# The first layer norm of an AdaLN block in its channel layout: row factors spread through DRAM in place of eight transposes, from the fourth batch on

## What is computed

```python
h = layernorm(x) * (1 + ca) + sa
u, gate = split(h @ W_in.T)
b_t  = u @ W_state.T
dt_t = minimum(softplus(u @ W_dt.T + b_dt), 10)
decay = exp(-dt_t * rate)
h_t = decay * h_t-1 + (1 - decay) * b_t          # scan over the 512 tokens
z = (h_t @ W_C.T) * silu(gate) + h * D
x = x + ga * (z @ W_out.T)
h = layernorm(x) * (1 + cb) + sb
xr, xk = mu_r * h + (1 - mu_r) * h_prev, mu_k * h + (1 - mu_k) * h_prev
x = x + gb * sigmoid(xr @ W_r) * (square(relu(xk @ W_k)) @ W_v)
```

## Time and profile before

| | us |
|---|---|
| median of 3 runs | 361.68 (361.56 to 362.54) |
| span of the profiled execution | 360.2 |
| PE busy | 353.1 (98%) |
| ACT busy | 306.8 (85%) |
| DVE busy | 302.7 (84%) |
| POOL busy | 256.5 (71%) |
| from scan to scan, batches 3 to 15 | 20.83 each |

### The profile page before, as it was taken

How to read it: one execution, slowest core, us unless ns; L and a number is a source line. 1 busy time by engine, 2 the same in 40 slices (tenths; PEclk the granted TensorE clock), 3 DMA queues, 4 the chain that set the end, 5 groups by cost and what they waited for, 6 DMA issues and landing times.

```text
span 360.2 us, 5599 instructions
## 1 busy us (share of the span) xinstructions
PE 353.1 (98%) x1680; PEld 277.3 (77%) x1680; DVE 302.7 (84%) x640; ACT 306.8 (85%) x422; POOL 256.5 (71%) x268
## 2 busy tenths in 40 slices
PE   8999899999999999999999999999999999999995
PEld 4667567788888888888888888888888888887654
DVE  3779997989989798988979898997989789768846
ACT  4677689799898989989898998989898998988484
POOL 2140849969696987969697796969789696766642
PEclk9999999999999999999999999999999999999999
DMA  8932130220413132040313104031301103010013
GB/s 289 405 119 70 46 119 0 88 90 0 136 40 116 59 104 74 13 146 18 118 60 116 60 35 139 4 116 59 119 0 58 61 0 118 0 61 1 0 58 117
DMA packets 13150, 29.15 MB, mean 81 GB/s; under 512 B 1216, under 2 KB 1984, under 8 KB 12992
## 3 DMA queue, kind: packets, MB, share of 16 engines
q1 hardware_dynamic: 12400, 28.32, 22.6%
q10 hardware_dynamic: 720, 0.48, 0.4%
HBM read 20.40 MB, written 8.39 MB: 80 GB/s over the span
## 4 chain that ended last, share of the span: by engine, by line
PE 91%; DVE 4%; ACT 2%; issue 2%; POOL 0%; ACTq 0%; DVEq 0%; POOLq 0%
PE slot L259 70%; PE slot L266 7%; PE slot L355 4%; PE slot L510 2%; PE slot L509 2%; PE slot L519 2%; PE slot L280 1%; PE slot L273 1%; ACT prev L636 1%; PE slot L363 1%; DVE xn L901 1%; PE slot L302 0%; DVE xk L935 0%; DVE stats L858 0%; DVE xr L935 0%
## 5 line engine op out<-in xcount | busy, mean ns | idle before, releaser
L1147 POOL TENSOR_TENSOR rstd<-mv,half_neg 128x4 f32<-128x4 f32 x16 | 16.1, 1009 | 44.8 <-DVE mv L873 44.8
L636 ACT ACTIVATE prev<-slot,mod,mix_prev 128x512 f32<-128x512 f32 x64 | 46.5, 790 | 1.1 <-PE slot L266 0.8
L259 PE MATMUL slot<-h_hi,wf_hi 128*128 128x512 f32 x120 | 44.0, 407 | 0.0
L1123 POOL TENSOR_TENSOR k_lo<-k_act,k_hi 128x512 fp32r<-128x512 f32 x30 | 38.2, 1297 | 7.7 <-ACT k_act L839 4.2
L1123 POOL TENSOR_TENSOR xk_lo<-xk,xk_hi 128x512 fp32r<-128x512 f32 x30 | 38.4, 1299 | 6.3 <-ACT xk_hi L664 6.3
L259 PE MATMUL slot<-h_hi,wf_lo 128*128 128x512 f32 x120 | 42.8, 397 | 0.0
L1166 POOL TENSOR_TENSOR h_lo<-h,h_hi 128x512 fp32r<-128x512 f32 x28 | 35.8, 1301 | 9.7 <-ACT h_hi L645 9.7
L1123 POOL TENSOR_TENSOR xr_lo<-xr,xr_hi 128x512 fp32r<-128x512 f32 x32 | 42.3, 1324 | 0.2 <-ACT xr_hi L670 0.2
L1217 POOL TENSOR_TENSOR z_lo<-z,z_hi 128x512 fp32r<-128x512 f32 x26 | 33.7, 1298 | 4.9 <-ACT z_hi L738 4.7
L957 DVE TENSOR_TENSOR slot<-silu,slot 128x1024 f32<-128x1024 f32 x16 | 19.7, 1230 | 20.0 <-PE slot L519 18.8
L259 PE MATMUL slot<-h_lo,wf_hi 128*128 128x512 f32 x120 | 35.1, 397 | 0.0
(11 more groups left out here) (157 smaller groups left out, 1009.7 us busy)
## 6 DMA issues: line engine op xcount, KB each, us to landing
x_ch<-x_ch_in SPq DMA_DIRECT2D x16, 512.0 KB, 3.8
x_tok<-x_tok_in SPq DMA_DIRECT2D x15, 512.0 KB, 3.5
x_out<-wmod SPq DMA_DIRECT2D x15, 512.0 KB, 3.0
wmod<-wmod_in SPq DMA_DIRECT2D x1, 1024.0 KB, 8.8
w_in<-weights_in SPq DMA_DIRECT2D x1, 1024.0 KB, 11.5
w_in<-weights_in SPq DMA_DIRECT2D x1, 512.0 KB, 4.5
wmod<-wmod_in SPq DMA_DIRECT2D x1, 512.0 KB, 5.7
x_tok<-x_tok_in SPq DMA_DIRECT2D x1, 256.0 KB, 3.2
```

Of the source, the lines that this page charges most:

```text
L259: ins = nc.tensor.matmul(out, w[:, c, at + d * P:at + (d + 1) * P], x[:, c, :], start=first, stop=last)
L636: return nc.scalar.activation(prev[:, mix, i, 1:T + 1], ps_n[:, i, :], ACT.Identity, bias=mod_at(SHIFT2 + i, k), scale=mix_prev[:, mix, i, ...
L1123: nc.gpsimd.tensor_tensor(lo, x, hi.bitcast(F32), ALU.subtract).then_inc(done, 1)
L1147: nc.gpsimd.tensor_tensor(rstd2[:, k % 2], mv2[:, k % 2, 1, :], half_neg[:], ALU.pow).then_inc(rstd2_ok, 1)
```

## The change

From batch 3 on (the fourth) the first norm is made in the channel layout:

- the tokens of `x_tok` of these batches lie interleaved in pairs, so that one bn_stats over 512 values gives the statistics of two tokens. DVE's `ln1_rows` is two such instructions; bn_aggr and DVE's and ACT's `ln1_apply` are gone;
- POOL's `ln1_rows` makes two values for each token from them, 1/root and mean/root, in three small instructions (`rows1`, 128x2x4);
- SP's `spread` writes these to DRAM as two rows of 512 and, when that has landed, reads them back to all 128 partitions (`spread_rows`, 128x2x512), two DMAs, between the load of `x_tok` and the store of a result;
- ACT's `offsets` makes `offset1` from the second row with the batch's scale and shift (two instructions, after the last rounding of xr and before the exponential); ACT's `modulated` is gone;
- DVE's `scaled` multiplies both halves of `x_ch` by the first row in one instruction over 128x1024 (into the memory of `xn1`), where `ln1_apply` stood, and DVE's `modulated` makes `h` from that and `offset1` in two instructions, between the second norm's `normalised` and `gated`. All three read two tiles in SBUF;
- PE's eight transposes of `first_norm` are gone for these thirteen batches; its wait for `z` stands ahead of the `dt` product instead;
- `x_ch` has three buffers, its loads come one batch earlier; `rv` and `r_last` share memory with the weights of the modulation.

```diff
+            def spread(k):
+                sp.wait_ge(rows_ok, k - WHOLE)
+                sp.dma_start(rows1_d[k].rearrange("h (p j) -> p h j", j=TT), rows1[:, k % 2]).then_inc(s_row_out, 16)
+                sp.wait_ge(s_row_out, 16 * (k - WHOLE))
+                if k - 2 > WHOLE:
+                    sp.wait_ge(offset_ok, k - 2 - WHOLE)
+                    sp.wait_ge(scaled1_ok, k - 2 - WHOLE)
+                sp.dma_start(spread_rows[:, k % 2], rows1_d[k].partition_broadcast(P)).then_inc(s_row_in[k % 2], 16)
...
-                if live(a):
-                    first_norm(a)
...
+            def offsets(k):
+                act.wait_ge(s_row_in[k % 2], 16 * ((k - WHOLE + 1) // 2))
...
+                for i in range(CH):
+                    last = nc.scalar.activation(offset1[:, i], spread_rows[:, k % 2, SHIFT], ACT.Identity,
+                                                bias=mod_at(SHIFT1 + i, k), scale=scale_neg[:, i, k:k + 1])
...
+            def ln1_rows(k):
+                before(dve, rows_ok, k - 2 - WHOLE)
+                for q in range(TT // 2):
...
+                    last = nc.vector.bn_stats(stats1[:, k % 2, q, :], x_tok[:, k % 3, 2 * q:2 * q + 2].rearrange("p a b -> p (a b)"))
...
+            def scaled(k):
...
+                nc.vector.tensor_tensor(scaled1, x_ch[:, k % 3], spread_rows[:, k % 2, RSTD:RSTD + 1].to_broadcast([P, CH, T]), ALU.mult).then_inc(scaled1_ok, 1)
...
+                for i in range(CH):
+                    last = nc.vector.scalar_tensor_tensor(h[:, k % 2, i], scaled1[:, i], scale_root[:, i, k:k + 1], offset1[:, i], ALU.mult, ALU.add)
...
+                if live(a) and a > WHOLE + 1:
+                    modulated(a)
                 if live(b):
                     gated(b)
...
                 if live(a + 1):
-                    ln1_apply(a + 1)
+                    scaled(a + 1)
                 if live(a):
                     clipped(a)
...
+            def ln1_rows(k):
+                pool.wait_ge(st1_ok, k + 1)
...
+                nc.gpsimd.tensor_scalar(spread1[:, k % 2, 1, :], tokens[:, :, 2], EPS * C, None, ALU.add).then_inc(row_spread_ok, 1)
...
+                nc.gpsimd.tensor_tensor(rows1[:, k % 2, RSTD], spread1[:, k % 2, 1, :], half_neg[:], ALU.pow).then_inc(row_rstd_ok, 1)
...
+                nc.gpsimd.tensor_tensor(rows1[:, k % 2, SHIFT], tokens[:, :, 1], rows1[:, k % 2, RSTD], ALU.mult).then_inc(rows_ok, 1)
```

More of the change, by code:

```diff
@@ L77, in adaln_block @@
         x_tok = sb("x_tok", [P, 3, TT, C])
-        x_ch = sb("x_ch", [P, 2, CH, T])
+        x_ch = sb("x_ch", [P, 3, CH, T])
         x1 = sb("x1", [P, 3, CH, T])
@@ L233, in _ @@
                 if live(a + 3) and live(a):
-                    sp.wait_ge(xn1a_ok, a + 1)
-                    sp.wait_ge(xn1b_ok, a + 1)
+                    if a <= WHOLE:
+                        sp.wait_ge(xn1a_ok, a + 1)
+                        sp.wait_ge(xn1b_ok, a + 1)
+                    else:
+                        sp.wait_ge(st1_ok, a + 1)
                     load_tokens(a + 3)
+                if live(a + 1) and a > WHOLE:
+                    spread(a + 1)
                 if live(d):
@@ L246, in _ @@
                         sp.dma_start(out_d[d, :P], x2[:, d % 2, 0]).then_inc(s_out[d % 2], 16)
-                if live(b) and live(b + 2):
+                if live(b) and live(b + 3):
                     sp.wait_ge(x1_ok[0], b + 1)
                     sp.wait_ge(x1_ok[1], b + 1)
-                    load_channels(b + 2)
+                    load_channels(b + 3)
+                if b == 0:
+                    spread(WHOLE + 1)
             sp.wait_ge(s_out[0], 16 * (NB // 2))
@@ L717, in _ @@
             nc.scalar.preload_act_table_set("natural_log_exp_and_others")
-            ln1_apply(3)
+            offsets(WHOLE + 1)
             act.wait_ge(mix_ok, 1)
@@ L740, in _ @@
                     rounded_xk(d, 0)
-                if live(b) and b > WHOLE:
-                    act.wait_ge(t1_ps, b + 1)
-                    act.wait_ge(z_ok[0], b - 1)
-                    act.wait_ge(z_ok[1], b - 1)
-                    modulated(b, 0)
                 if 0 < d < LAST:
@@ L748, in _ @@
                 if live(b) and b > WHOLE:
-                    modulated(b, 1).then_inc(h_ok, 1)
                     rounded_h(b)
@@ L756, in _ @@
                     rounded_xr(d, 1)
+                if live(a) and a > WHOLE + 1:
+                    offsets(a)
                 if live(b):
@@ L768, in _ @@
                         nc.scalar.preload_act_table_set("silu_and_others")
-                if live(a) and a > WHOLE + 1:
-                    ln1_apply(a)
                 if split_state(b) and b > WHOLE:
@@ L1044, in _ @@
             normalised(0)
-            ln1_stats(4)
-            ln1_apply(3)
+            ln1_rows(4)
             mixing(0, 0)
@@ L1054, in _ @@
             normalised(1)
-            ln1_mean_variance(4)
+            scaled(WHOLE + 1)
+            modulated(WHOLE + 1)
             for s in STEPS:
@@ L1169, in _ @@
             ln1_scale(1)
+            pool.wait_ge(mod1_ok, 1)
+            nc.gpsimd.tensor_scalar(scale_neg[:], mod[:, SCALE1:SCALE1 + CH, :], -float(np.sqrt(C)), None, ALU.mult)
+            nc.gpsimd.tensor_scalar(scale_root[:], mod[:, SCALE1:SCALE1 + CH, :], float(np.sqrt(C)), None, ALU.mult).then_inc(root_ok, 1)
             weight_low_part(1, MIX_K)
@@ L1201, in _ @@
                     low_state(b)
-                if live(a + 1) and d > 0:
-                    ln1_scale(a + 1)
+                if live(a + 1):
+                    ln1_rows(a + 1)
                 if live(d) and d < LAST:
```

69 lines of the change are left out of this document (48 added, 21 removed).

## The result

| | before | after |
|---|---|---|
| median, us | 362.54 (361.56 to 363.27, 5 runs) | 365.15 (364.71 to 365.89, 5 runs) |
| ratio to before | | 1.0071, 95% interval [1.0046, 1.0095] |
| span of the profiled execution, us | 360.2 | 363.1 |
| scan to scan, batches 4 to 14, us | 20.83 | 21.00 |
| step to batch 3, us | 21.82 | 23.13 |

What follows compares the result with a forecast made beforehand. PE, without a gap, was taken to set the 20.84 us step. Eleven steps +5.8, the last -0.3, the step to batch 3 +2.0: +7.5 on the span, median 369.2 us; forecast's range 366 to 373, 8 in 10 runs 357 to 377.

Steps and rivals of the forecast that it cites:

- the power did not get between: Rival: POOL's power runs before DVE's second `modulated`, delaying `gated`; 1.26 us a step, 378 us; chance 0.10.
- the last step has no price: Step to batch 15: no `scaled` there, so 0.3 us shorter.
- The rival without exclusion: Rival: DVE's two-SBUF-tile instructions and POOL's do not matter to each other; steps 20.53, 358.2 us; chance 0.20.
- the one-sided: Rival: DVE waits for POOL, POOL never for a two-tile instruction; +0.06 us a step, 363.6 us; chance 0.12.
- the size of three turns: POOL's tensor_scalar behind first `modulated`, power behind the second, `xr_lo` behind `scaled`: each charged whole; step 21.37 us.
- 11 x 0.53: Eleven steps, ending with the scans of batches 4 to 14, each 0.53 us longer: +5.8 us.
- My lower bound, 0.32: Per step: the two `modulated` cost POOL nothing, `z_lo` waits for `z_hi` until +8.18; 0.32 us longer.
- The upper bound's 0.75: Per step: two-tile streaming of 0.60 for 512 columns in place of 0.53, four times; 0.75 us longer.
- The step to batch 3: Prologue's end: `scaled` and two `modulated` come ahead of `gated`; 1.0 to 2.9 us late, taken as +2.0.
- The ring without the port: Step without SBUF exclusion between DVE and POOL: PE takes `z_hi` of half 1 0.31 us earlier, 20.53 us.
- The clip was to show 1.2: Sign that the forecast is right: DVE's clip lasts near 1.2 us in place of 0.43, ending just behind `xr_lo`.
- PE was to be idle 1.4 a step: Sign that the forecast is right: PE idles about 1.4 us a step, ahead of the state product, `k_lo` and `z_hi`.

Runs made afterwards that it cites:

- the runs that take the price away: On the kernel after: `xr_lo` of half 0 waits for the clip, 0.9972 of before; or `scaled` reads one SBUF and one PSUM tile, 0.9971.

## Why the prediction was right in sign and three times too large

**Right.** PE stops being the bound; `scaled` is held to the end of `h_lo`, `xr_lo` goes behind `scaled` (2.27, forecast near 2.4), the clip behind `xr_lo`; POOL's wait for `z_hi` has shrunk from 0.39 to some 0.04; `gated` starts at +3.16, so the power did not get between; the offsets, the rows' two DMAs and the third buffer cost nothing; the last step has no price. The rival without exclusion fell with the runs that take the price away, the one-sided with `xr_lo`'s 2.27.

**The step that failed: the size of three turns.** Where GpSimd waits for VectorE, the working let its instruction begin when the turn came and charged it its whole duration. The rows show it begun before, and it ended 0.13 to 0.15 us sooner than that:

| | forecast | measured | charged too much |
|---|---|---|---|
| tensor_scalar of the rows, end | +2.80 | +2.67 | 0.13 |
| second `modulated`, end | +3.33 | +3.24 | (0.09 passed on) |
| power to `k_lo`, start of `k_lo` | +4.60 | +4.36 | 0.15 more, 0.24 in all |
| `h_lo`, end | +14.71 | +14.48 | the same 0.23 |
| `scaled`, end | +15.78 | +15.56 | 1.08 for 1.07, nothing |
| `xr_lo`, end | +17.08 | +16.71 | 1.15 for 1.30, 0.15 more |
| clip, end | +17.36 | +16.99 | 0.28 for 0.28, nothing |
| next scan's end | +21.37 | +21.00 | 0.37 in all |

The power shows it best: it started at 227.35, while the second `modulated` ran to 227.78, and ended 0.89 behind that; alone it takes 1.04. The tensor_scalar, 0.23 alone, ended at 227.20, 0.09 behind the first `modulated`:

```profile
226.25 0.87 DVE L945 SCALAR_TENSOR_TENSOR h<-xn,scale_root,offset 128x512 f32<-128x512 f32 x1
```

Whether GpSimd does those 0.13 to 0.15 us ahead of its turn, or VectorE gives up the port that much before its row ends, no run tells apart. For the clip I had made that deduction (0.28 of 0.43), for POOL's instructions not, and the trace of the kernel before already had it. The `xr_lo` of the earlier trace rows ends at 196.31, 1.15 behind the first of the two L895 beside it, where a subtraction alone takes 1.30:

```profile
194.75 0.41 DVE L895 TENSOR_SCALAR xn<-x_tok,rstd,shift 128x256 f32<-128x256 f32 x1
```

A further row agrees: in the kernel with the rows behind `k_lo`, the pair of `k_lo` started 0.53 before the end of `modulated` and lasted 0.40 longer than 2.55. So 11 x 0.17 (and 0.16 once) stands in place of 11 x 0.53: 3.7 of the 4.6 us between 7.5 and 2.9. My lower bound, 0.32, has `z_lo` of half 1 wait for `z_hi` until +8.18, and it does, until +8.16; it left out the same deduction for `xr_lo`, and less 0.15 it is what was measured. That is in part luck: the bound supposed that the two `modulated` cost POOL nothing, while they cost it 0.36, which the idle 0.39 ahead of `z_lo` happened to take up. (The upper bound's 0.75 is 0.81 by its own terms, 0.53 and four times 0.07; the end of the range stays at 373.)

**The step to batch 3** cost 1.31 where I took 2.0. By the timelines of that step `gated` starts at +5.38 for +2.86 before, 2.5 late and within my bounds; but I passed its lateness on as the step's. `h_lo` ends only 0.84 later (+16.61 for +15.77), since the row had slack between, and the port adds 0.47.

**A rival's size.** The ring without the port was put at 20.53. It is 20.70 to 20.74: the working took `z_hi` for the next wait behind PE's work, read its margin at a product and not at the weight load ahead of it, and did not count the wait for VectorE's `xk` at all, which is the one that ends last (0.09 of room). Had nothing excluded anything, the change would have brought 0.1 a step, some 1 us and not that rival's 3.5.

**Signs that misled.** The clip was to show 1.2 and shows 0.65, because it is called later (+16.34 for +16.17) and released earlier. PE was to be idle 1.4 a step; by the row of its matmuls it has hardly a gap, and the waits stand at the weight loads (17.2 us in the three lines above that name an engine, and 8 us more under "issue" than before).

**Left open.** Where the 0.35 us of start and tail come from; 0.24 of them lie ahead of the first scan, which starts anywhere from 16.38 to 17.20 us in the traces of these kernels, so they are within what one execution of these differs from another. And why one of the eleven steps is 0.16 longer: DVE stands 0.20 between two small instructions of the second norm, and nothing in the profile is waited for. The same step, to batch 9, is 0.14 to 0.18 longer in nine of the eleven other kernels made from the one after and in none made from the one before, so it belongs to the program.
